# Cross attention and gene routing on one core: eight first iterations and the last ones written out in an order of each engine's own

## The reference

```python
x = x + xattn(layernorm(x), ctx, pos, pos, Wq, Wkv, Wout, bout)
x = x + ffn(layernorm(x), Wc, temperature, genes, Wd, Wu, norm_w, scale)

# xattn: 32 heads of 16, keys and values from a context of 128 x 256
q = rope(x @ Wq, pos);  k, v = split(ctx @ Wkv);  k = rope(k, pos)
w = softmax(einsum('bqhd,bkhd->bhqk', q, k) / 4)
out = einsum('bhqk,bkhd->bqhd', w, v) @ Wout + bout

# ffn: 1024 genes, the 32 best per token
xn = rmsnorm(x) * norm_w
top_vals, top_idx = top_k(xn @ Wc.T / clip(temperature, 0.1), 32)
expressed = softmax(top_vals) @ genes[top_idx]            # 64 numbers a token
out = tanh(expressed @ Wd.T) * xn * (expressed @ Wu.T) * scale
```

## Time and profile before

| | us |
|---|---|
| median of three runs | 510.07 |
| the profiled execution | 507.2 |
| its span, first to last instruction | 505.4 |
| PE busy in the span | 432.6 |
| DVE busy | 386.5 |
| ACT busy | 273.5 |
| POOL busy | 257.3 |

### The profile page before, as it was taken

How to read it: one execution, slowest core, us unless ns; L and a number is a source line. 1 busy time by engine, 2 the same in 40 slices (tenths; PEclk the granted TensorE clock), 3 DMA queues, 4 the chain that set the end, 5 groups by cost and what they waited for, 6 DMA issues and landing times. The chain is left out here.

```text
span 505.4 us, 11005 instructions
## 1 busy us (share of the span) xinstructions
PE 432.6 (86%) x3866; PEld 341.5 (68%) x3866; DVE 386.5 (76%) x611; ACT 273.5 (54%) x418; POOL 257.3 (51%) x263
## 2 busy tenths in 40 slices
PE   0645778989999999999999999999999998885824
PEld 0534456768888888787777777777778776673613
DVE  4584143698989898989888888888989888868470
ACT  3661626474757575757575757565757563542211
POOL 1363535556666666666666665657474753031121
PEclk9987689999999999999999999999999998998857
DMA  7931324140414141414141404141323222000000
GB/s 246 325 69 28 76 64 87 32 93 25 96 44 95 45 95 46 93 43 93 43 94 32 101 27 100 35 93 42 82 53 75 61 56 51 2 22 0 21 21 21
DMA packets 82027, 34.45 MB, mean 68 GB/s; under 512 B 73152, under 2 KB 75216, under 8 KB 82000
## 3 DMA queue, kind: packets, MB, share of 16 engines
q1 hardware_dynamic: 81040, 33.05, 27.8%
q10 hardware_dynamic: 960, 1.05, 0.7%
HBM read 12.86 MB, written 4.19 MB: 34 GB/s over the span
## 5 line engine op out<-in xcount | busy, mean ns | idle before, releaser
L400 POOL TENSOR_TENSOR stage_b<-stage_b,cos_t 128x512 f32<-128x512 f32 x32 | 40.9, 1279 | 111.3 <-issue 60.1
L855 DVE TENSOR_REDUCE row_max<-psum 128x8 f32<-128x1024 f32 x64 | 75.4, 1220 | 19.7 <-PE psum L1150 19.3
L917 DVE MAX8 top<-stage_b 128x8 f32<-128x1024 f32 x64 | 78.5, 1226 | 12.1 <-ACT stage_b L636 9.7
L926 DVE MATCH_REPLACE8 stage_b<-top,stage_b 128x1024 f32<-128x1024 f32 x64 | 77.5, 1211 | 0.6 <-issue 0.3
L446 POOL TENSOR_TENSOR down<-down,kept 128x512 f32<-128x512 f32 x16 | 20.6, 1290 | 105.7 <-ACT down L665 105.7
L636 ACT ACTIVATE stage_b<-psum,rstd 128x512 f32<-128x512 f32 x32 | 22.0, 688 | 83.7 <-PE psum L1073 83.7
L600 ACT ACTIVATE stage_a<-psum 128x1024 f32<-128x1024 f32 x64 | 63.5, 1022 | 0.0
L1073 PE MATMUL psum<-wcT_h,yT_h 128*128 128x512 f32 x128 | 54.2, 424 | 4.0 <-DVE yT_l L903 3.2
L1073 PE MATMUL psum<-wcT_l,yT_h 128*128 128x512 f32 x128 | 51.5, 402 | 0.0
L1073 PE MATMUL psum<-wcT_h,yT_l 128*128 128x512 f32 x128 | 51.1, 399 | 0.0
L1194 PE MATMUL psum<-stage_a,v_ext 128*32 128x128 f32 x1024 | 38.0, 284 | 3.6 <-ACT stage_a L600 3.0
(11 more groups left out here) (128 smaller groups left out, 1038.8 us busy)
## 6 DMA issues: line engine op xcount, KB each, us to landing
x_ring<-x_dram SPq DMA_DIRECT2D x16, 256.0 KB, 2.6
out_dram<-x_ring SPq DMA_DIRECT2D x16, 256.0 KB, 2.0
ctx_sb<-ctx_dram SPq DMA_DIRECT2D x16, 128.0 KB, 2.6
stage_a<-L_ffn_Wc_dram SPq DMA_DIRECT2D x1, 2048.0 KB, 11.1
stage_b<-L_xattn_Wq_dram ACTq DMA_DIRECT2D x1, 1024.0 KB, 5.7
stage_b<-L_xattn_Wkv_dram SPq DMA_DIRECT2D x2, 512.0 KB, 9.0
stage_b<-L_xattn_Wout_dram SPq DMA_DIRECT2D x1, 1024.0 KB, 13.5
genes_sb<-L_ffn_genes_dram SPq DMA_DIRECT2D x2, 256.0 KB, 5.2
```

The lines of the kernel that those rows point to most:

```text
L400: pool.tensor_tensor(halves(qk_cos), halves(qk_sb), trig(cos_t, t), ALU.mult).then_inc(s_cosm[n], 1)
L855: nc.vector.tensor_reduce(row_max[:, 0:HEADS].rearrange("p (odd m) -> p odd m", odd=2)[:, :, 4 * g:4 * g + 4], score_of[g][:].rearrange("p ...
L917: nc.vector.max(top[:, 8 * n:8 * n + 8], logit if n == 0 else rest).then_inc(s_top[n], 1)
L926: nc.vector.match_replace(rest, top[:, 8 * n:8 * n + 8], logit if n == 0 else rest, REMOVED).then_inc(s_rem[n], 1)
```

## The change

**Orders.** `run` now takes three functions from each engine: `filling`, written out step by step, in place of iterations 0 to 7; `iteration(i)`, the loop's list, for i from 8 to 15 on every engine, in the same order as before; and `draining`, written out, for the rest. In PE, ACT and POOL the index counts one higher, so that their first loop turn works on the same tiles as before, and the loop has eight turns instead of nine; tile 15's projections are in `draining`. In `filling` and `draining` each engine has an order of its own, no longer the full iteration's. Some waits are moved or added accordingly, a few also in PE's loop list, where two groups of `scoresT`, `values`, the second half of `transpose_w` and `down_up` now name a semaphore of their own; the loop has eight register instructions on PE where it had nine.

**Setup.** x of tile 0 is the first load of ACT's queue. SP no longer waits for it before the large loads, and issues x of tile 1 and the context of tile 1 right behind the genes. `ctx_hi(0)` is ACT's first step; PE transposes the context of tile 1 before it transposes `Wc`, and projects k of tile 1 ahead of the first scores. `wcT` uses other PSUM banks and its last quarter, `Wout`'s two parts (`wout_hi`, `wout_lo`) move behind tile 0's scores or exponentials. A one-element exponential (`warm_exp`) takes ACT's table load for the exponentials forward into the setup; another table load comes ahead of ACT's first copy.

**Staging.** `stage_b` is 4096 wide instead of 6144 and a third area `stage_c` of 2048 holds `Wout` first, then `kept`, `down` and `yn`; the tensors are spread otherwise over the areas.

**First queries.** Rotation, sum and low split of tile 0's queries run on DVE (`rope_q0`, `rope_sum_q0`, `split_lo_q0`) instead of POOL; the keys stay on POOL.

The core of the diff (the lists of `filling` and `draining` are shown in part, those of the other engines are of the same kind):

```diff
-        def run(eng, lags, iteration, counts=()):
-            def tiles(i):
-                return [i - n if 0 <= i - n < TILES else None for n in range(lags)]
-            for i in range(lags + 1):
-                iteration(*tiles(i))
-            with eng.Fori(lags + 1, TILES) as i:
+        def run(eng, filling, iteration, draining, counts=()):
+            filling()
+            with eng.Fori(8, TILES) as i:
                 for n in counts:
                     eng.to_reg(i - n)
-                iteration(*(i - n if n else i for n in range(lags)))
-            for i in range(TILES, TILES + lags - 1):
-                iteration(*tiles(i))
+                iteration(i)
+            draining()
...
             sp.dma_start(pos_raw[:], pos.rearrange("t p c -> t (p c)")).then_inc(s_pos, 16)
-            load_x(0)
             load_ctx(0)
...
-            sp.wait_ge(s_x, 16)
-            load_x(1)
             sp.dma_start(wc_raw, wc.rearrange("(g p) d -> p g d", p=P)).then_inc(s_wc, 16)
...
+            def filling():                          # of SP
+                next_x(1)
+                next_ctx(1)
+                next_x(2)
+                turn(0, 1)
+                turn(0, 0)
...
+            act.dma_start(slot(0), x[0]).then_inc(s_x, 16)
             act.dma_start(wq_raw, wq.rearrange("(k p) n -> p k n", p=P)).then_inc(s_wq, 16)
...
+            def rope_q0():
+                dve.wait_ge(s_trig, 1)
+                dve.wait_ge(s_q_sb, 1)
+                nc.vector.tensor_tensor(halves(qk_cos), halves(qk_sb), trig(cos_t, 0)[:, 0:2 * HEADS], ALU.mult).then_inc(s_cosm[0], 1)
+                nc.vector.tensor_tensor(halves(qk_sin), halves(qk_sb), trig(sin_t, 0)[:, 0:2 * HEADS], ALU.mult).then_inc(s_sinm[0], 1)
...
+            def filling():                          # of PE
+                transpose_pos()
+                transpose_ctx(0)
+                transpose_x(0)
+                project_k(0)
+                project_v(0)
+                transpose_ctx(1)
+                wcT(0)
+                wcT(1)
+                project_q(0)
+                wcT(2)
+                project_k(1)
+                transpose_x(1)
+                duT()
+                project_q(1)
+                scores(0, 2)
...
+                values(0, 0)
+                scoresT(0, 3)
+                scoresT(0, 2)
+                values(0, 1)
+                values(0, 2)
+                project_q(2)
...
+            def draining():                         # of PE
...
+                logits(13, 1)
+                transpose_attn(14)
+                scoresT(15, 0)
+                scoresT(15, 1)
+                transpose_w(12, 0)
+                transpose_w(12, 1)
+                scoresT(15, 2)
+                project_out(14)
...
+                express(15)
+                down_up(15, 0)
+                down_up(15, 1)
```

1330 lines of the change are left out of this document (1015 added, 315 removed).

## The result

| | before | after |
|---|---|---|
| median of 4 runs, us | 509.87 (509.35 to 510.09) | 494.68 (494.34 to 494.88) |
| profiled execution, us (span) | 507.2 (505.4) | 494.34 (492.5) |
| DVE's first maximum of tiles 0 to 3, us | 42.98, 66.01, 89.39, 113.64 | 43.8, 63.8, 86.5, 109.9 |
| first maximum of tile 6, then of tile 15 | 189.4, 419.7 | 188.1, 417.9 |
| from tile 15's first maximum to the end | 85.7 | 74.6 |

A forecast was written before the change was run, and what follows sets the result against it. PE was taken to bound the middle, with its gaps at the two ends. The terms summed to -11 for the start and -11 for the end, -22, so 510.07 - 22 = 488 us; range 478 to 499.

The forecast's parts named there:

- Setup: Before the first scores: DVE's first maximum of tile 0 at 41.4 instead of 42.98, -1.5 us, bounds -4 and +1.
- the last issue (genes) ends at 22.7 - 3 = 19.7: SP's load queue at the start: without the wait for x, the large loads come about 3 us sooner.
- Tile 1: Second tile of the start: its first maximum at 60.5 instead of 66.01, -5.5 us in all.
- two turns cost about 2 + 4.8 us: Second tile of the start: time for the two turns, behind the exponentials, before its first maximum at 60.5.
- Tile 2: Third tile of the start: turn at 74.3, first maximum at 79.7 instead of 89.39, -9.7 us.
- PEclk full from the second tile on: Sign to look for in the start: PE's granted clock full from the second tile on.
- Tile 3: Fourth tile of the start: PE fills up, 22.6 us between maxima, 102.3 instead of 113.64, -11; bounds -5 and -17.
- From there to the loop: Between tile 3's first maximum and the loop: same work in the lists, PE full already, so 0 us.
- In the loop: The loop's turns: same order, added waits already over, 0 us, bounds +2 to -2 over eight turns.
- The end: Last tiles behind the loop: earlier `project_out` and last selection, together -11 us, bounds -6 and -14.
- the bracket of 493 to 503: Case for the whole time: the fill stays a chain or the context lands late; chance 0.23.
- the end alone is shorter: Rival: context lands near 30, +5 us in setup eats most of the fill, 494; within the 0.23 case.

## Why the prediction was right in the end and wrong in the start

**Setup: forecast -1.5, measured +0.8.** The failed step is "the last issue (genes) ends at 22.7 - 3 = 19.7". SP's wait for x had not delayed the later issues by its own length: inside the burst the issues themselves are long, whenever they are reached (the genes' two 2.87 us after, 3.07 before, against 0.43 for the context's behind them). They ended at 21.5, 1.2 us earlier and not 3. From issue to landing the context took 3.7 us, between the 2.6 and 5.2 that were weighed, so it landed at 26.4 instead of 24. `read_q(0)` then started at 33.0 instead of 30: behind the context stand six steps of ACT and not the seven that were counted, but they and PE's steps between took 6.7 us, not 6, at a granted clock of 0.74 (7.5 us at 0.66 in the run with iterations 6 and 7 in the loop's order, whose first maximum came at 44.7). From there to the first maximum it was 10.8 us instead of 11.4. So the first maximum came 2.4 us late (43.8 against 41.4), as late as the context, with two smaller misses that cancel. The 2 us put for the rotation on DVE were right (33.97 to 36.1); by the run with the rotation on POOL the move is worth 3.1 us at the first maximum.

**Tile 1: forecast 19.1, measured 20.0.** The gain was right in kind: the stretch is 3.0 us shorter than before, all of it ahead of the exponentials, because `project_k(1)` and the table load behind it are out of the way. They start 8.5 us after the first maximum where 9.4 were forecast. The failed term is what follows, 11.5 us from there to the next maximum where 9.7 were put. SP issues the two turns at 55.53 and 57.75, and PE resumes at

```profile
63.38 0.62 PE L1675 MATMUL psum<-kT,qT 64*128 64x128 f16 x16 [0.98 <-DMA qT<-parts]
```

which makes 2.2 + 5.6 us for "two turns cost about 2 + 4.8 us"; the first also went out 0.9 us later behind the exponentials than taken.

**Tile 2: forecast 19.2, measured 22.7.** This is the largest miss. The keys' last transpose went out at 81.15, 17.3 us after tile 1's maximum, where 13.8 were forecast; from there it took 5.3 (forecast 5.4). 1.9 to 2.0 us are the one POOL product beside `wout_lo`, shown by moving it. I had put "`wout_lo` is out of DVE's way" to the good and not asked what its new place would meet. The Trainium skill (SBUF — State Buffer, SBUF: two separate sides) says that an instruction of DVE with two SBUF inputs and one of GpSimd that reads SBUF can't run together: the one that starts first holds the shared ports to its end. The trace agrees: the product, begun at 72.31, would have been held till 74.40, 2.1 us, and took 1.96 more than alone. Where POOL came first, DVE's subtraction took 3.25 us instead of 2.28. About 1.0 of the other 1.5 us is the low clock of PE between 67.2 and 71.3 us, ahead of the keys' rotation: the three runs without it had 21.7 us, though POOL was held up there too. The forecast had "PEclk full from the second tile on"; this stretch shows 0.92. The last 0.5 us is not resolved, nor is why the clock fell in some runs and not in others.

**Tile 3: forecast 22.6, measured 23.4.** PE had 23.27 us of work there, where 22.6 were taken; its gaps did go.

**From there to the loop: forecast 0, measured +2.4.** The failed sentence is "the lists hold the same work and PE is full already". PE is full in the loop's order (25.29 of 25.3 us in the stretch shown); the written-out order leaves 2.7 us of short gaps in 78.2. The run with iterations 6 and 7 in the loop's order took them back.

**In the loop: forecast 0, measured 0** (154.8 against 154.9 for six turns; 0.5 us less from tile 6 to tile 15).

**The end: forecast -11, measured 85.7 - 74.6 = -11.1.** Step by step, counted from tile 15's first maximum, which the forecast left at 419.7 and which came at 417.9: `project_out(15)` starts after 31.2 us where 31.9 were forecast (37.9 before) and took 3.1 us at the high clock (forecast 2.8); the last selection starts after 48.8 us, as forecast (57.5 before); in it `combine(14)` no longer waits and the selection up to `mask(15)` takes 11.3 us instead of 13.2 (forecast -1.5, measured -1.9); from there to the end 14.5 instead of 14.9 (forecast -0.5, measured -0.4). That the drain's order is the cause is shown by both exchanges of the drain. That it hangs on the places of `attn_lo(15)` and its neighbours on DVE is shown by putting six steps back, which costs 14 us; the forecast's share for `attn_lo(15)` alone, -6, was not tested by itself (`project_out(15)` started 4.8 us later in that run).

**The sum.** -11 for the start (102.3 against 113.64, so -11.3) became -1.3 at the loop's entry, 10.0 us short by the terms above: 2.4, 0.9, 3.5, 0.8 and 2.4; the end held. With 0.5 us in the loop that is 12.9 us from profiled execution to profiled execution. The medians differ by 15.2, since the profiled execution of the kernel before was one of its quicker ones. The forecast carried the 2.9 us between that execution and the median over to the new time; the changed kernel has only 0.3 there, and no run shows why. With the traces' 12.9 us alone the forecast's sum would end at 497, still in the range. So the time came into the range by the end, which was right, with nine tenths of the start missing, and by some 2.5 us of luck. The time fell into the bracket of 493 to 503, which had 0.23. The rival that came nearest is "the end alone is shorter" at 494: its price was right and its reason half (the context landed at 26.4, not near 30, and the fill lost the rest in two other places).

## What to carry to other kernels

In this fill, where each tile's transfer waits for the last tile's result, a delay at the start passed whole to the end. Moving the one load that all engines waited for ahead of the bulk loads in its queue gave 7 to 8 us, more than all reordering of the fill. So look first for the stretch in which all engines stand idle, and at what ends it. Once PE was full, the loop's settled order was better than the written-out one, and handing over to it two tiles sooner took the gaps out. In the drain, a short step on which PE's next long step depends went into a wait ahead of a block of long steps, not inside the block. Where the order of one engine is changed, the others must follow: one engine's old order beside another's new one undid the whole gain here.
